# One order change in an attention loop on all five queues, and a bias operation on GpSimd cut in two

## The reference, cut to what matters

```python
xn = layernorm(x, g_in)
q = (xn @ Wq).reshape(b, n, H, DH).transpose(0, 2, 1, 3) * scale
kv = xn @ Wkv                      # one key and one value head for all 16
...                                # a null key and value in front: 257 keys
sim = einsum('bhid,bjd->bhij', q, k) + bias
sim = where(causal, neg, sim); sim = where(mask, sim, neg)
attn = softmax(sim)
out = einsum('bhij,bjd->bhid', attn, v).transpose(0, 2, 1, 3).reshape(b, n, 1024) @ Wo
return layernorm(out, g_out)
```

## Time and profile before

| | |
|---|---|
| median of 3 runs | 849.12 us (839.8 to 855.49) |
| the profiled execution | 854.32 us |
| its span in the profile | 852.6 us |
| PE busy | 737.8 us, 87% |
| DVE busy | 476.1 us, 56% |
| POOL busy | 422.6 us, 50% |
| ACT busy | 361.0 us, 42% |

### The profile page before, as it was taken

One profiled execution on the slowest core, in us unless ns is written; L12 is line 12 of the kernel. 1 busy time (PEld: TensorE's weight loads), 2 busy tenths in 40 slices (PEclk: granted clock), 3 DMA queues, 4 the chain that ended last, 5 costly groups with the idle time before them and its releaser, 6 DMA issues. The chain is left out here.

```text
span 852.6 us, 15701 instructions
## 1 busy us (share of the span) xinstructions
PE 737.8 (87%) x4481; PEld 568.2 (67%) x4482; DVE 476.1 (56%) x1751; ACT 361.0 (42%) x1068; POOL 422.6 (50%) x506
## 2 busy tenths in 40 slices
PE   8859995966999989985899989899989688988788
PEld 5349964655999989863566656566666445877665
DVE  2704464464232222246778899988989742444346
ACT  3526621233222222245546655565656315665302
POOL 1166315414453863245638486867857431344530
PEclk9889997966999999998999999999999778999979
DMA  9634533325979666188977777778868743444346
GB/s 315 257 99 143 136 111 112 100 87 166 351 255 356 215 180 205 56 296 309 336 260 246 240 237 249 253 249 265 264 205 273 237 148 96 119 122 139 107 142 197
DMA packets 101035, 173.41 MB, mean 203 GB/s; under 512 B 10976, under 2 KB 77792, under 8 KB 99936
## 3 DMA queue, kind: packets, MB, share of 16 engines
q1 hardware_dynamic: 79392, 117.03, 41.7%
q0 software_dynamic: 10944, 30.03, 11.5%
q10 hardware_dynamic: 10624, 25.46, 8.7%
HBM read 111.86 MB, written 60.62 MB: 202 GB/s over the span
## 5 line engine op out<-in xcount | busy, mean ns | idle before, releaser
L2181 POOL TENSOR_TENSOR work<-work,region_ac 128x386 f32<-128x386 f32 x128 | 119.4, 941 | 69.3 <-ACT work L1693 32.9
L1706 ACT ACTIVATE work<-work 128x129 f32<-128x129 f32 (+1 forms) x256 | 114.2, 448 | 89.2 <-DVE work L1838 87.3
L1863 DVE STREAM_TRANSPOSE region_bd<-work 128x384 f32<-128x384 f32 x128 | 73.3, 572 | 12.2 <-ACT work L1706 6.3
L1515 PE MATMUL psM<-region_ac,work 128*128 128x256 f32 x256 | 71.1, 403 | 9.7 <-DVE acc L1881 9.7
L1504 PE MATMUL psL<-region_bd,work 128*64 128x256 f32 (+1 forms) x512 | 61.6, 365 | 19.0 <-DMA region_bd<-c_blocks 17.0
L1367 POOL DMA_INDIRECT d_pairs<-work,home x47 | 45.9, 976 | 64.0 <-DVE home_f L1119 44.9
L1477 PE MATMUL psY<-work,region_ac 128*128 128x256 f32 x256 | 71.3, 401 | 2.2 <-ACT work L1700 2.2
L1504 PEld LDWEIGHTS psL<-region_bd,work 128*64 128x64 f32 x512 | 34.1, 147 | 55.1 <-DMA region_bd<-c_blocks 27.2
L1356 POOL DMA_INDIRECT b_pairs<-work,home x39 | 38.1, 977 | 56.9 <-DVE work L1063 54.6
L860 PE MATMUL psH<-work,region_bd 128*128 128x128 f32 x472 | 62.8, 290 | 3.9 <-ACT work L968 2.2
L1348 POOL DMA_INDIRECT work<-in_x,inv x39 | 37.1, 953 | 55.5 <-DVE inv L1276 35.0
(11 more groups left out here) (367 smaller groups left out, 1608.3 us busy)
## 6 DMA issues: line engine op xcount, KB each, us to landing
c_blocks<-region_bd SPq DMA_DIRECT2D x64, 512.0 KB
region_bd<-c_blocks SPq DMA_DIRECT2D x64, 512.0 KB
region_bd<-in_b_w ACTq DMA_DIRECT2D x37, 512.0 KB
work<-d_rows SPq DMA_DIRECT2D x47, 132.0 KB
a_slots<-work SPq DMA_DIRECT2D x19, 256.0 KB
region_bd<-in_b_w SPq DMA_DIRECT2D x1, 4096.0 KB, 15.4
region_bd<-in_d_w SPq DMA_DIRECT2D x1, 4096.0 KB, 19.7
work<-d_pairs SPq DMA_DIRECT2D x16, 256.0 KB
```

The source lines that it names most:

```text
L1515: last = pe.matmul(psM[:, i * DIM:(i + 1) * DIM], c_oT[:, j % 2, i * P:(i + 1) * P], c_wo[:, j, :], start=(j == 0 and i == 0), stop=(j == ...
L1706: nc.scalar.activation(c_p[:, j % 2, o, a:z], c_sc[:, o, a:z], ACT.Exp, scale=-1.0, bias=c_min[:, o, i:i + 1], accum_out=c_sum[:, j % 2, o ...
L1863: nc.vector.transpose(out=c_x1[:, p % 2, :, (QT + 1) * o:(QT + 1) * (o + 1), :].rearrange("p b i q -> p i b q"), in_=c_p[:, j % 2, o, 1:1 ...
L2181: pool.tensor_tensor(c_bm[:, 2 * (j % 2) + o, :], c_mp, c_bias[:, 2 * j + o, :], ALU.subtract).then_inc(C.bm_ready, 1)
```

## The change

On every queue of attention some steps change places, one buffer is added, and POOL's bias operation is cut in two.

- `c_oT` has three buffers instead of two; `dve_o` waits for `pe_out` of one pair earlier than before.
- PE: `pe_out` of a batch's first pair is not issued at the end of iteration j = 4, but in iteration j = 5 after `pe_sum`.
- ACT: `act_normal_rows` (j = 3) comes after the second exp instead of before the queries; `act_zT` (j = 2) before the second exp instead of at the end.
- DVE: `dve_o` comes right after the first scores; the dispatch steps and `dve_row_shift` come before the second scores; row moments and variances move from the start of j = 3 to the end of j = 2; `dve_dest` moves from j = 2 to 1, `dve_best` and `dve_onehot` move one j later, with the last two both at j = 7.
- POOL: `pool_row_rstd` comes inside j = 3, after the first head; each `pool_bm` is two operations, of 129 and 257 columns, the second of which signals.
- SP: load p directly follows store p.

```diff
-            work, [..., DIM, 512, KEYS, 24, 1024, 2 * QT * DH, 4])
+            work, [..., DIM, 3 * SEQ, KEYS, 24, 1024, 2 * QT * DH, 4])
@@ pe_batch
                 if s >= 0:
                     pe_sum(pe, s, s % NPAIR, s // NPAIR)
+                if j == 5:
+                    pe_out(pe, 8 * b, 0, b)
...
-                if s >= 1:
+                if s >= 1 and j != 4:
                     pe_out(pe, s - 1, (s - 1) % NPAIR, (s - 1) // NPAIR)
@@ act_batch
-                if j == 3 and not last:
-                    act_normal_rows(act, b + 1)
                 if j == 4 and not last:
                     act_rowsT(act, b + 1, 1 - odd)
                 if not (last and j + 3 >= NPAIR):
                     act_queries(act, p + 3, j + 3)
+                if j == 2 and b >= 2:
+                    act_zT(act, b - 2)
                 if more:
                     act_exp(act, p + 1, j + 1, ORDER[1])
+                if j == 3 and not last:
+                    act_normal_rows(act, b + 1)
...
-                if j == 2 and b >= 2:
-                    act_zT(act, b - 2)
@@ dve_o
-            wait(dve, C.wo_mm, p - 1)
+            wait(dve, C.wo_mm, p - 2)
@@ dve_dispatch
-            if j == 2 and b >= 3:
                 dve_dest(dve, b - 3)
...
-            if j == 4 and b >= 2:
+            if j == 5 and b >= 2:
                 dve_best(dve, b - 2, 0)
-            if j == 5 and b >= 2:
+            if j == (5 if last else 6) and b >= 2:
                 dve_onehot(dve, b - 2, 0)
-            if j == (5 if last else 6) and b >= 2:
+            if j == (5 if last else 7) and b >= 2:
                 dve_best(dve, b - 2, 1)
-            if j == (5 if last else 7) and b >= 2:
                 dve_onehot(dve, b - 2, 1)
@@ dve_batch
-                if j == 3 and not last:
-                    dve.wait_ge(C.row_step, 4 * b + 6)
-                    dve_row_moments(dve, b + 1)
-                    dve_row_variances(dve, b + 1)
                 if more:
                     dve_scores_wait(dve, p + 1)
                     dve_scores(dve, p + 1, j + 1, ORDER[0])
+                if s >= 0:
+                    dve_o(dve, s, s % NPAIR)
                 dve_blocks(dve, p, j, ORDER[1])
                 dve_sums(dve, p, j)
                 dve_recs(dve, p)
-                if s >= 0:
-                    dve_o(dve, s, s % NPAIR)
...
+                dve_dispatch(dve, b, j, last)
+                if j == 3 and not last:
+                    dve_row_shift(dve, b + 1)
                 if more:
                     dve_scores(dve, p + 1, j + 1, ORDER[1])
+                if j == 2 and not last:
+                    dve.wait_ge(B.combined, 2 * b + 4)
+                    dve_row_stats(dve, b + 1)
+                    dve.wait_ge(C.row_step, 4 * b + 6)
+                    dve_row_moments(dve, b + 1)
+                    dve_row_variances(dve, b + 1)
...
-                dve_dispatch(dve, b, j, last)
@@ pool_bm
-            pool.tensor_tensor(c_bm[:, 2 * (j % 2) + o, :], c_mp, c_bias[:, 2 * j + o, :], ALU.subtract).then_inc(C.bm_ready, 1)
+            for a, z in ((0, KEYS0), (KEYS0, KEYS)):
+                last = pool.tensor_tensor(c_bm[:, 2 * (j % 2) + o, a:z], c_mp[:, a:z], c_bias[:, 2 * j + o, a:z], ALU.subtract)
+            last.then_inc(C.bm_ready, 1)
@@ sp_attention
             for p in range(pairs):
                 sp_store_blocks(sp, p)
-                if p >= 1:
-                    sp_load_blocks(sp, p - 1)
-            sp_load_blocks(sp, pairs - 1)
+                sp_load_blocks(sp, p)
```

More of the change, by code:

```diff
@@ L318, in build @@
         (c_xn, c_xnT, c_qr, c_bm, c_sc, c_p, c_nullo, c_oT, c_mp, c_small, c_gat, c_v, c_rec) = carve(
-            work, [512, 1024, 512, 4 * KEYS, 2 * KEYS, 4 * KEYS, DIM, 512, KEYS, 24, 1024, 2 * QT * DH, 4])
+            work, [512, 1024, 512, 4 * KEYS, 2 * KEYS, 4 * KEYS, DIM, 3 * SEQ, KEYS, 24, 1024, 2 * QT * DH, 4])
         c_gat = c_gat.rearrange("p (r c n) -> p r c n", r=QT, c=2)
@@ L329, in build @@
         c_p = c_p.rearrange("p (r o n) -> p r o n", r=2, o=2)
-        c_oT = c_oT.rearrange("p (r n) -> p r n", r=2)
+        c_oT = c_oT.rearrange("p (r n) -> p r n", r=3)
         c_min = c_small[:, 0:4].rearrange("p (o i) -> p o i", o=2)
@@ L1514, in pe_out @@
             for i in range(QT):
-                last = pe.matmul(psM[:, i * DIM:(i + 1) * DIM], c_oT[:, j % 2, i * P:(i + 1) * P], c_wo[:, j, :],
+                last = pe.matmul(psM[:, i * DIM:(i + 1) * DIM], c_oT[:, p % 3, i * P:(i + 1) * P], c_wo[:, j, :],
                                  start=(j == 0 and i == 0), stop=(j == NPAIR - 1), skip_group_check=True)
@@ L1870, in dve_o @@
             wait_dma(dve, C.blocks_loaded, 0, p)
-            wait(dve, C.wo_mm, p - 1)
-            nc.vector.tensor_tensor(c_oT[:, j % 2, :].rearrange("p (i a q) -> p i a q", i=QT, a=4),
+            wait(dve, C.wo_mm, p - 2)
+            nc.vector.tensor_tensor(c_oT[:, p % 3, :].rearrange("p (i a q) -> p i a q", i=QT, a=4),
                                     psL[:, 0:SEQ].rearrange("p (i a q) -> p i a q", i=QT, a=4),
@@ L2103, in dve_batch @@
                 dve_recs(dve, p)
-                if s >= 0:
-                    dve_o(dve, s, s % NPAIR)
                 if j == 4 and not first:
                     dve_out_raw(dve, b - 1)
-                if j == 2 and not last:
-                    dve.wait_ge(B.combined, 2 * b + 4)
-                    dve_row_stats(dve, b + 1)
                 if j == 5 and not first:
@@ L2120, in dve_batch @@
                     dve_out_stats(dve, b - 1)
-                if j == 3 and not last:
-                    dve_row_shift(dve, b + 1)
                 if j == 5 and not first:
                     dve_out_shift(dve, b - 1)
-                dve_dispatch(dve, b, j, last)
         def dve_attention(dve):
@@ L2265, in pool_batch @@
                         pool_pairs(pool, b + 1, h)
+                    if j == 3 and n == 0 and not last:
+                        pool_row_rstd(pool, b + 1)
                     if j == 4 and n == 0:
@@ L2278, in pool_batch @@
                         pool_dispatch(pool, b - 2, 2 * n + 1)
-                if j == 3 and not last:
-                    pool_row_rstd(pool, b + 1)
         def pool_biases(pool, t):
```

## The result

The changed kernel takes 924.45 us (median of 4 runs, 923.04 to 925.88). The kernel before takes 846.79 (median of 4, 839.8 to 855.49). The ratio is 1.0947, with a 95% interval of 1.0869 to 1.1026: slower by 78 us, where 16 us less were forecast and 848 was the upper end of the range.

A forecast was written before the change was run, and what follows sets the result against it. PE and DVE were near their limit, neither at it. Gains of 3.0 us in each of four batches (2.6 + 0.7 - 0.3), plus 2.0, 1.5 and 0.5, gave 16 us: 849.1 to 833, range 821 to 848.

The forecast's parts named there:

- the term for SP: SP's load behind its own store: zero for the first batch (4 us lost to 3 gained), no delay seen later.
- Rival B: The wait only moves, to `dve_o` or SP's stores; 2 of 3 us a batch come back, 843 us; chance 0.18.
- stores issued over 1 us after the last recs: On SP's queue: a sign that would show the forecast wrong.
- The split: POOL's bias in two operations: 0.1 us per extra start, 1.6 us more a batch (0.8 to 5.0), 0.3 let through.
- The shorter hold: Shorter POOL bias pieces hold up DVE's small operations less: 0.7 us a batch off DVE.
- rival D: The split does not shorten POOL's hold of DVE; 4 us missing, 837 us; counted within the forecast's 0.60.
- Rival C: POOL becomes the bound if the extra start costs 0.3 us; 18 us more, 867 us; chance 0.09.
- The term for PE: First pair's `pe_out` behind `pe_sum` of j = 5: its 1.90 us wait goes, and mostly the clock's 1.4 us.
- 35 to 36 us a batch: Attention's windows from the fourth to the seventh batch: the length that would show the forecast right.
- `dve_o`'s early place brings a wait of its own: On DVE: a new wait on `pe_sum` of more than 0.3 us a pair would show the forecast wrong.

The follow-up runs named there:

- e1: The changed kernel with SP's old order (store p, then load p - 1); 796.44 us, 1.005 of before.
- e2: The kernel before with SP's new order alone (load p right behind store p); 871.8 us, 1.1003 of before.
- e13: e10 with the two `best` and two `onehot` steps at their new j (5, 6, 7, 7); 847.98 us, 0.9996 of before.
- e12: e10 with `dve_dest` at its new j = 1; 836.9 us, 0.9898 of before.
- e10: The changed kernel with SP's old order, whole bias operation, and routing steps behind the second scores at their old j; 839.04 us, 0.981 of before.
- e4: The kernel before with POOL's bias in two operations, nothing else; 799.94 us, 1.01 of before.
- e3: e1 with the bias as one operation of 386 columns; 792.29 us, 1.0025 of before.
- e14: The kernel before with only the first pair's `pe_out` moved to j = 5 and the third `c_oT`; 838.57 us, 0.9899 of before.
- e11: e10 with `dve_o` back at its old place behind blocks, sums and recs; 834.32 us, 0.9835 of before.
- e15: e10 with block loads from the seventh pair on issued by ACT; 840.14 us, 0.9921 of before.
- e8: The changed kernel with each load from the third pair on reading half its bytes; 852.27 us, one run.
- e7: The changed kernel with each store from the fifth pair on writing half its bytes; 879.92 us, one run.
- e5: e3 with block loads from the seventh pair on issued by ACT, SP only storing after that; 1.003 of before.
- e6: The kernel before with block loads from the seventh pair on issued by ACT, nothing else; 0.997 of before.

## Why the prediction was wrong

**The step that failed** is the term for SP: "it goes out up to an iteration earlier, but the next store stands behind it", then "From the second batch on, no load shows this" and "I take zero for the first batch". The wait was named and its price was taken from the wrong order. With the old order a store stands ahead of the load and lands in 2.9 us (e1). The change puts it 0.47 us behind one, and there it lands in 5.4 (e2). That landing then stands between a store and its own load, and the load between that and the next store: 0.47 + 5.3 us = 5.8 a pair, against the 4.8 that a pair took before (38.3 / 8). 8 x 1.0 = 8 us a batch, where zero stood in the sum. Rival B had the right place ("SP's queue holds stores back where transfers are dense") and priced it at 2 us a batch at most, with the DMA share as its condition. A ring of latencies needs no dense transfers: the share fell to 0.60. The warning was at hand: the prediction itself said that a store had taken over 6 us to land (the earlier trace rows have the load that waited for it), and called it a trouble of the first batch, when an iteration is 4.8 us and a landing longer than that was enough to set the pace. Nor was it the first batch alone: in the second a load went out at 428.07, 1.69 us after the store ahead of it, though that one may have waited for `dve_o`, which ended at 427.66. One sign of being wrong that the prediction names, stores issued over 1 us after the last recs, did come: 3.6 us in the ring above.

**The time of the routing steps was not in the sum at all.** The diff moves `dve_best` and `dve_onehot` by one iteration, and the second two together into j = 7. This costs 1.0% (e13 against e12; 1.1% by attention against e10), as much as all the rest of the order brings. The rows had even shown j = 7, 0 and 1 full, PE busy 10.88 and DVE 10.66 of 10.90 us; the prediction asked what each step's place in the iteration costs and not what its iteration holds.

**The split** was taken at 0.1 us a head, with 0.8 to 5.0 us a batch as the range. It measured 0.19 us, so 3.0 us a batch of work; POOL's busy time rose by 2.3 to 2.5. The shorter hold was right in its kind and its size: about 1 us a batch comes off DVE (33.4 against 34.2 to 34.6) where 0.7 was taken, and the median of one such line fell from 928 to 386 ns in e4, so rival D falls. The sum was wrong in sign: 0.7 less 0.3 us a batch was to be a gain, and it costs 1.0% (e4). Rival C "begins to hurt above 0.15 us a start", and 0.19 is above it, but its price of 18 us was for 0.3 us a start: 8 us were lost. In the changed order, e1 against e3, the split's cost is 0.0025 with overlapping intervals, so there it isn't shown. Which wait carries it in e4 stays open.

**The term for PE was right.** No wait of `pe_out` for `dve_out_raw` is left, e14 gains 1.0% by this step alone, and the clock is 1.00 over whole batches in e11. 35 to 36 us a batch were forecast from the fourth to the seventh, and e11 has 34.55 to 35.51; its attention is 15.1 us shorter, where 16 were forecast. e11 has neither SP's new order, nor the split, nor the new iterations of the routing steps, nor the early `dve_o`. So the gain was sized right for another set of edits, and that is in part luck: the 16 us held 0.4 us a batch for the split, which costs time, and nothing for the routing steps. That `dve_o`'s early place brings a wait of its own was named as a sign to look for: it does (16.5 us, 23 times, in e10; 12.6, 5 times, in e11 and 13.0, 5 times, before), 0.26 us a pair and so under the 0.3 named, and it costs nothing that the times can tell.

**The best version** is e11, 1.7% below before and 10% below the changed kernel; e10 and it can't be told apart. The intervals of e10, e11, e12, e14 and e15 don't reach 1.

## What to carry to other kernels

When two transfers of one queue depend on each other, draw the ring before pricing an order: what each needs landed, what stands behind it, and how long a transfer takes *in its new place*, with the bytes ahead of it. If the sum over the ring is above an iteration, that sum is the new period, however idle the DMA engines are. A landing time read in one order need not hold in the other: here it was 2.9 us in one and 5.4 in the other.

When a diff moves steps in two ways, inside the iteration and from one iteration to another, price both; here only the second could be seen in the times. A list of busy shares by iteration shows which ones have room.

## What the runs showed of the hardware

A 512 KB store issued 0.47 us behind a 512 KB load on SP's queue lands 5.4 us after its issue (median, e2), and 2.9 us when it goes out ahead of the load (e1). From its issue to that of its own load are 5.25 us; 3.85 with half the load's bytes (e8), 4.64 with half its own (e7). With the loads on ACT's queue the whole kernel gains nothing over SP's old order (e5, e6, e15). An operation of POOL on two SBUF operands costs about 0.19 us to start a second time (129 and 257 columns: 438 + 689 ns; 386 columns: 941). The line through the two pieces has 1.96 ns a column and 0.19 us at none; the prediction's two lines, from other operations, gave 0.05 and 0.31 us.
